# The second batch's row bias moved from ScalarE to VectorE, and one small matmul moved a step earlier, in a fused attention and mixture-of-experts kernel

## What is computed

```python
lam = LAMBDA_MAX * exp(-ALPHA * u_prev)
use_sparse = lam >= SPARSE_THRESHOLD
scores = einsum('bhqd,bhkd->bhqk', Q, K) * scale
dense_out  = softmax(scores + lam * where(prior_mask, 0.0, -1.0)) @ V
sparse_out = softmax over the 32 keys listed for each query, with multiplicity
out = where(use_sparse, sparse_out, dense_out)
```

## Time and profile before

| | |
|---|---|
| median of three runs | 1662.32 us |
| the profiled execution | 1662.16 us |
| its span, first to last instruction | 1660.4 us |
| PE / DVE / ACT / POOL busy, share of the span | 94% / 52% / 44% / 42% |
| mean granted PE clock, of full speed | 0.964 |
| first attention | about 115 to 660 us |
| stretch in which ACT makes the bias of batch 1 | 297.6 to 357.2 us |

### The profile page before, as it was taken

One profiled execution on the slowest core, in us unless ns is written; L12 is line 12 of the kernel. 1 busy time (PEld: TensorE's weight loads), 2 busy tenths in 40 slices (PEclk: granted clock), 3 DMA queues, 4 the chain that ended last, 5 costly groups with the idle time before them and its releaser, 6 DMA issues. The chain is left out here.

```text
span 1660.4 us, 20515 instructions
## 1 busy us (share of the span) xinstructions
PE 1558.2 (94%) x7392; PEld 762.5 (46%) x7392; DVE 869.0 (52%) x2041; ACT 734.8 (44%) x998; POOL 696.3 (42%) x515
## 2 busy tenths in 40 slices
PE   5789999989999999899999888999999999999998
PEld 3423333323333333333433334555656577777755
DVE  7578878888678855557765733342422111111141
ACT  4754666766566665476645566223211111111111
POOL 4437999987799998143210120400001200000070
PEclk9559999999999999999998898999999999999999
DMA  3551033243231310344532015100040005243071
GB/s 97 143 155 33 24 80 76 70 98 78 60 85 35 79 46 8 79 117 109 125 73 64 28 33 166 61 0 0 0 152 4 22 1 183 92 162 114 16 129 24
DMA packets 75905, 121.43 MB, mean 73 GB/s; under 512 B 14920, under 2 KB 53265, under 8 KB 72731
## 3 DMA queue, kind: packets, MB, share of 16 engines
q1 hardware_dynamic: 72155, 113.62, 24.3%
q0 software_dynamic: 3072, 6.03, 2.1%
q10 hardware_dynamic: 576, 0.47, 0.1%
HBM read 85.08 MB, written 36.96 MB: 74 GB/s over the span
## 5 line engine op out<-in xcount | busy, mean ns | idle before, releaser
L1141 POOL TENSOR_TENSOR sb_prob<-sb_prob,sb_weight 128x1024 f32<-128x1024 f32 x192 | 448.0, 2357 | 44.6 <-ACT sb_prob L1355 44.1
L1355 ACT ACTIVATE sb_prob<-wide 128x1024 f32<-128x1024 f32 (+3 forms) x384 | 347.5, 916 | 207.9 <-PE wide L1965 109.1
L1960 PE MATMUL wide<-sb_stack_q,sb_stack_k 99*128 99x512 bf16 (+3 forms) x896 | 282.8, 364 | 16.2 <-ACT sb_prob L1355 7.4
L1399 ACT ACTIVATE sb_sil<-wide 128x320 f32<-128x320 f32 (+1 forms) x128 | 66.2, 517 | 436.0 <-PE wide L2039 436.0
L1644 DVE CUSTOM_DVE_ANT_0 sb_junk<-bank,sb_bias 128x512 bf16<-128x512 f32 x339 | 226.8, 688 | 61.7 <-PE bank L1933 57.0
L1933 PE MATMUL bank<-sb_stack_k,sb_stack_q 96*128 96x512 bf16 (+3 forms) x597 | 217.3, 380 | 17.1 <-DVE sb_rowmax L1638 5.8
L2039 PE MATMUL wide<-sb_weight,sb_ffn 128*128 128x512 f32 x512 | 232.3, 597 | 0.0
L1980 PE MATMUL wide<-sb_prob,sb_v_aug 128*17 128x512 f32 (+3 forms) x1792 | 221.2, 560 | 7.6 <-ACT sb_o_raw L1368 6.2
L1638 DVE TENSOR_REDUCE sb_rowmax<-bank 128x1 f32<-128x512 f32 (+3 forms) x258 | 139.2, 559 | 88.3 <-PE bank L1936 57.1
L1771 DVE TENSOR_TENSOR sb_act_s<-sb_sil,wide 128x512 f32<-128x512 f32 x64 | 43.9, 687 | 253.3 <-ACT sb_sil L1399 253.3
L1179 POOL DMA_INDIRECT sb_weight<-slots_out,sb_slot_r x32 | 31.5, 984 | 285.0 <-issue 283.2
(11 more groups left out here) (272 smaller groups left out, 1831.7 us busy)
## 6 DMA issues: line engine op xcount, KB each, us to landing
sb_stack_k<-parts SPq DMA_DIRECT2D x32, 256.0 KB, 6.8
o_raw<-sb_o_raw SPq DMA_DIRECT2D x32, 256.0 KB, 2.3
sb_big<-rg SPq DMA_DIRECT2D x8, 1024.0 KB, 4.9
sb_big<-ru SPq DMA_DIRECT2D x8, 1024.0 KB, 7.3
sb_big<-rd SPq DMA_DIRECT2D x8, 1024.0 KB, 10.7
sb_stack_q<-parts SPq DMA_DIRECT2D x16, 384.0 KB, 4.9
parts<-sb_o_norm SPq DMA_DIRECT2D x40, 128.0 KB
sb_stack_q<-parts SPq DMA_DIRECT2D x16, 256.0 KB, 5.4
```

What stands on the lines that cost most here:

```text
L1141: e.tensor_tensor(p, p, weight_of(*u[1:]), ALU.mult).then_inc(weigh_p.handle, 1)
L1355: e.activation(p[:, :, first:HALF], sc[:, :, first:HALF], ACT.Exp).then_inc(SC.empty_sem(u), 1)
L1399: e.activation(sil[:, i % 2, 0:n], SC.tile(u)[:, 0:n], ACT.Silu).then_inc(silu_a.handle, 1)
L1960: i = e.matmul(sc[:, j * HALF + first:(j + 1) * HALF], stack_k[0:ROWS_M, n % 3, g, kt * P:(kt + 1) * P], stack_q[0:ROWS_M, n % 3, g, half ...
```

## The change

It has four parts.

1. `kb` of batch 1 is done by DVE, with the instruction that batch 0 used already (is the count zero? times the flag), reading the loaded buffer `tab`. ACT's eight instructions (L1309) and the semaphore `bias_a` go; all who waited for it wait for DVE's.
2. The bias has the other sign (-1e30 instead of 1e30), and the `max` instruction adds it where it subtracted it.
3. One DVE instruction of 128x2 at the start (L1458, the positive flag) goes.
4. `listed` stands 4 units behind its `pv` instead of 5, in the plan and so on PE and DVE; 16 steps.

```diff
-  late += [(i, ("kw_load", 1, kt, half)), (i + 3, ("kw", 1, kt, half)), (i + 5, ("listed", 1, kt, half))]
+  late += [(i, ("kw_load", 1, kt, half)), (i + 3, ("kw", 1, kt, half)), (i + 4, ("listed", 1, kt, half))]
...
   (SP, kb_load)
-  w.wait_ge(bias_a.after((b, t - 2)))
+  w.wait_ge(bias_d.after((b, t - 2)))
...
   (ACT)
-  elif kind == "kb" and u[1] == 1:
-      _, b, t = u
-      w.wait_ge(tab_in[t % 2].after(("kb_load", b, t)))
-      w.wait_ge(flag_d.after("cap"))
-      w.wait_ge(BK.emptied(MAXES[NQ - 1][-1]))
-      e.activation(bias[:, t, :], tab[:, t % 2, :], ACT.Relu, bias=fl[6][:, b:b + 1],
-                   scale=fl[5][:, b:b + 1]).then_inc(bias_a.handle, 1)
...
   (DVE)
-  e.tensor_scalar(fl[6], fl[3], -NEG, None, ALU.mult).then_inc(sf, 1)
...
-  w.wait_ge((bias_a if b else bias_d).after((b, qt)))
+  w.wait_ge(bias_d.after((b, qt)))
...
   e.tensor_tensor_reduce(out=junk[...], in0=BK.tile(u)[...], in1=bias[:, qt, lo:hi], scale=1.0, scalar=-3e38,
-      op0=ALU.subtract, op1=ALU.max, accum_out=acc)
+      op0=ALU.add, op1=ALU.max, accum_out=acc)
...
-  elif kind == "kb" and u[1] == 0:
+  elif kind == "kb":
       _, b, t = u
-      w.wait_ge(SC.emptied(("turn_count", t)))
-      w.wait_ge(SC.filled(COUNTED))
-      e.tensor_scalar(bias[:, t, :], count_row[TURNS.index(t) % ROW_BUFS], 0.0, fl[6][:, b:b + 1],
+      if b:
+          w.wait_ge(tab_in[t % 2].after(("kb_load", b, t)))
+          w.wait_ge(BK.emptied(MAXES[NQ - 1][-1]))
+      else:
+          w.wait_ge(SC.emptied(("turn_count", t)))
+          w.wait_ge(SC.filled(COUNTED))
+      e.tensor_scalar(bias[:, t, :], tab[:, t % 2, :] if b else count_row[TURNS.index(t) % ROW_BUFS], 0.0, fl[5][:, b:b + 1],
                       ALU.is_equal, ALU.mult).then_inc(bias_d.handle, 1)
```

More of the change, by code:

```diff
@@ L758, in build @@
         flag_a = signal("act_flag", ["exp_u", "exp_lam"])
-        flag_d = signal("dve_flag", ["lam", "sparse", "dense", "neg", "pos", "cap", "keep", "rest"])
+        flag_d = signal("dve_flag", ["lam", "sparse", "dense", "neg", "cap", "keep", "rest"])
         index_d = signal("dve_index", ["copy", "neg", "wrap", "clamp"] + list(range(1, NT)) +
@@ L763, in build @@
         tables_a = signal("act_tables", of("kw"))
-        bias_d = signal("dve_bias", [u[1:] for u in of("kb") if u[1] == 0])
-        bias_a = signal("act_bias", [u[1:] for u in of("kb") if u[1]])
+        bias_d = signal("dve_bias", [u[1:] for u in of("kb")])
         weight_p = signal("pool_weight", [(*u[1:], z) for u in of("kw_sum") for z in ("sum",)])
@@ L1269, in _ @@
                     elif (att, b) == (1, 0):
-                        w.wait_ge(bias_a.after((1, NT - 1)))
+                        w.wait_ge(bias_d.after((1, NT - 1)))
                         w.wait_ge(BK.filled(OUTS[0, 0][-1]))
@@ L1457, in _ @@
             e.tensor_scalar(fl[5], fl[3], NEG, None, ALU.mult).then_inc(sf, 1)
-            e.tensor_scalar(fl[6], fl[3], -NEG, None, ALU.mult).then_inc(sf, 1)
             e.tensor_scalar(fl[2], fl[2], SPARSE_THRESHOLD, None, ALU.min).then_inc(sf, 1)
-            w.wait_ge(flag_d.after("pos"))
+            w.wait_ge(flag_d.after("neg"))
             w.wait_ge(load["cb"].end)
@@ L1645, in _ @@
                         out=junk[:, i % 2, 0:hi - lo], in0=BK.tile(u)[:, 0:hi - lo], in1=bias[:, qt, lo:hi], scale=1.0, scalar=-3e38,
-                        op0=ALU.subtract, op1=ALU.max, accum_out=acc).then_inc(BK.empty_sem(u), 1)
+                        op0=ALU.add, op1=ALU.max, accum_out=acc).then_inc(BK.empty_sem(u), 1)
                 elif kind == "fin" and u[2] == 0:
```

## The result

The changed kernel takes 1677.78 us (median of 11 runs, 1673.51 to 1681.63), the kernel before in the same comparison 1666.51 us (1662.16 to 1672.35). The ratio is 1.0064, with a 95% interval of 1.0048 to 1.008: slower by 10.7 us, 8.0 to 13.3. The profiled execution took 1676.56 us with a span of 1674.8. The forecast was +4.4 us and a range up to 1672.0.

The account below looks back on a forecast made before the run. POOL was taken to set the pace in 297 to 332 us, PE following with 1.06 us to spare. Terms 3.8 + 0.5 + 0.4 - 0.3 = 4.4 us on 1662.16 gave 1666.6 us, range 1660.5 to 1672.

Parts of the forecast that it names:

- The bounds of the wait: Each DVE bias step beside POOL waits for the rest of one POOL instruction: 0 to 2.36 us, taken as 1.18.
- Rival C: DVE becomes the bound: each step starts behind a fresh POOL instruction and costs 2.85 us; +18.8, 1681 us; chance 0.05.
- The wait of the other steps: Five steps ahead of 331 us: 8.35 us on DVE, of which 3.8 left, the middle of 2.7 and 4.9.
- PE's spare time and the lead: In 297 to 332 us, PE's spare 1.06 us and ACT's lead over POOL of 2.4 us absorb 3.5 us.
- Rival B: No wait between DVE and POOL: the five steps' 2.45 us are hidden; 1661.7 us; chance 0.2.
- Sixth and seventh step hidden, the eighth +0.5: Sixth hidden in PE's 2.96 us wait, seventh in DVE's idle time behind it; eighth costs 1.67, gives back 1.1.
- the hole: PE's 2.96 us wait for counts until 343.14 us, with half clock afterwards; claimed to hide the sixth step.
- `listed`, +0.4: Near 343 us, five matmuls move behind PE's wait, 2.1 us, against 1.0 and 0.7 us: +0.4.
- The sign: In the `max` instruction on DVE, adding the negative bias instead of subtracting costs nothing.
- ACT's relief: ACT loses eight instructions, 9.8 us in all; gains of 0.3 at 314, 0.7 at 347.18 and 1.1 us at 357.06.

Follow-up runs that it names:

- e10: e1 with a 0.14 us gap on POOL ahead of each of the two multiplications behind the first DVE step's request; +9.2 us on the kernel before.
- e1: The changed kernel with `listed` put back to 5 units behind; +10.5 us on the kernel before.
- e9: e1 with 0.14 us gaps on POOL ahead of five multiplications that run before and at the first DVE step's request; +7.2 us on the kernel before.
- e12: e10 with e7's two loads of counts queued ahead of the stack loads; +3.7 us on the kernel before.
- e13: e10 unchanged, measured again with more rounds; +3.8 us (1.2 to 6.3) on the kernel before.
- e6: Separate kernel: six gapless POOL multiplications, one DVE instruction of varying form asked as the first ends; plain `tensor_scalar` held for one POOL instruction of 2.1 us.
- e11: e1 with the steps in the accumulating form over 256 of 1024 columns; +0.5 us on the kernel before.
- e7: The kernel before with the first two loads of counts queued on SP ahead of the stack loads; 6.2 us faster, ratio 0.9963.
- e2: The kernel before with only `listed` one unit earlier; -0.8 us.
- e4: The kernel before with only the first of batch 1's eight bias steps on DVE; +8.7 us.
- e3: The kernel before with seven of batch 1's eight bias steps on DVE, the first left on ACT; +9.7 us.
- e8: Separate kernel: 22 gapless POOL multiplications, a DVE step asked at various places; 2.44 us behind the 4th, 8th and 12th, 13.94 behind the 16th.
- e14: Separate kernel: POOL runs with other request places, half-wide instructions, gaps or an earlier DVE entry; steps took from 2.38 us to 24.48 us.

## Why the prediction was wrong, by its own steps

**The bounds of the wait: this step failed.** The forecast took the wait for POOL as "the rest of a POOL instruction ..., from 0 to 2.36", half of it in the middle. Rival C, its worst case, gave each step one whole instruction. No row of the trace before showed a fast DVE instruction asking late in a long gapless run: L1606 asked at 31.03 us, when POOL's queue was short. Yet the row that spoke of it was there, 21 multiplications without a gap; I read it as "POOL sets the pace" and not as "POOL never lets go". Measured, the first step took 6.69 us. e10 against e1 puts that at 9.1 - 4.0 = 5.1 us of lag, most of the 6.3 us from the forecast 4.4 us to the 10.7 measured.

**The wait of the other steps: right, the 3.8 us partly by luck.** With the long hold gone (e10) the five steps ahead of 331 us took 2.05, 1.91, 0.48, 0.78 and 2.18 us, 7.4 in all for the 8.35 forecast, and the lag at 335 us was 4.0 us (3.7 to 5.1 in e9, e12 and e13) for the 3.8 forecast. But the 3.8 was the middle of two sums, 2.7 and 4.9, and nothing in the forecast says why the middle. That the instruction is like L1606 and unlike L1592 was the right choice: e6 has it held for 2.23 us beside L1606's form with 2.49.

**PE's spare time and the lead: used up at once.** The forecast had 3.5 us to take from. Its lead of 2.4 us was read off one pair; over the stretch in the kernel before it goes from 0.08 us (at 314 us, where POOL waits) to 4.07 us. A hold of 6.2 us beyond the step's own time broke through in one piece: PE stood 6.00 us, POOL 4.26, and the clock fell. Until the 65th multiplication (304.4 us before) the lag was 4.5 us, until the 71st 7.7 us: the 3.2 us between came with no lead left, as POOL's further idle times of 1.27, 0.81, 0.54 and 0.76 us show, and only up to 312 us at low clock. The forecast had no term for a fall of the clock ahead of 331 us.

**Rival B, no cost without a wait: right as a sum.** e11 measures it, +0.5 us (-1.7 to 2.8) for the -0.5 that it gave (1661.7 against 1662.16). Only its premise is false.

**Sixth and seventh step hidden, the eighth +0.5: right in this trace.** The changed kernel's lag grows from 9.2 to 10.0 us behind 335 us (the eighth step's 1.67 - 1.1 is 0.57; nothing hangs on it). In e13's trace it grows by 3.7. e12 bears out that the hole hides something: without it the growth from e7's lag is 5.8 us, in which the last three steps are not told from what the fifth left behind.

**`listed`, +0.4: not to be told from nothing.** e2 has -0.8 us (-4.5 to 2.7), and e1 and the changed kernel differ by 0.2. The longer stand of PE, and its being made up, is as described in e2 (4.67 us). In the changed kernel, which comes there late, PE stands for the counts only 2.11 us, at 354.78.

**The sign: right.** The maxima take as long as before, against 688 ns in the earlier trace rows:

```profile
L1635 DVE CUSTOM_DVE_ANT_0 sb_junk<-bank,sb_bias 128x512 bf16<-128x512 f32 x340 | 227.0, 687 | 58.6 <-PE bank L1928 56.0
```

**ACT's relief** was not measured by itself. In e11, where no step waits for POOL, it and the 0.4 us steps on DVE come out even.

The change is within 1%, as forecast, but above the range. The range ended where one POOL instruction per step ends; it should have had a case in which the lock isn't given back at each boundary.

**Open.** Why DVE got in ahead of the small instruction L1130 at 304.35 us in the changed kernel, though POOL seems to have no pause there. e4 does the same; in e1 DVE gets in only behind that instruction, when POOL runs dry, and in e3 two such boundaries pass. So "until POOL pauses" isn't the whole rule. And whether e10's two times, +9.2 and +3.8 us, are scatter or a difference in how the loads of the hole fell: that was seen in the lags, not forced.

## What to carry to other kernels

Before a copy, a cast, a plain `tensor_scalar` or anything with two SBUF inputs is put on DVE, look at POOL's timeline at that place: a row with a count of 16 or more and no bracket means that the instruction may stand until that row ends, however short it is. Two cautions: a run can go on through several rows without a bracket, and a row can hide pauses of 0.14 us, so compare its length with its count. Use a form that isn't held (an input in PSUM, or the accumulating form, here 1.21 us for 0.49), or give POOL a pause of 0.14 us just behind the place by a wait for its own last instruction (that freed the step here; what it gave back in the kernel's time, +9.2 and +3.8 us for +10.5, is not settled). And price a stand of PE at more than its length where all engines run in step: here the 6.00 us at 305 us had become a lag of 7.7 us some 15 us later, and closing the hole of 2.96 us at 343 us gave 6.2. The half clock and the lost lead behind such a stand are the likely rest.

## What was not expected of the hardware

- In a gapless run POOL gives DVE its turn at the next instruction boundary when DVE asks during one of the first 15 instructions, and not when it asks from the 16th on: steps of 2.37 us against 6.97, 13.94 and 24.48 us. In e8 and e14 only a pause ended the hold; in the changed kernel and in e4 it ended one small instruction earlier. The count is of instructions, not of time (held at an age of 24.6 us with half-wide ones, let in at 32.4 us with whole ones). A pause (0.14 us was enough in the kernel) or DVE's own entry sets it back.
- A fast DVE instruction over only 64 columns is held as long as one over 1024: 1.98 and 2.23 us in e6.
- In a short burst the turns go both ways: POOL beside four fast DVE instructions lost 0.35 us (2.47 for 2.12), and the next DVE instruction stood for POOL, 2.61 us in all. A long gapless run of DVE against POOL was not tried.
